# Feed-forward: the rounding offset finished by a second ScalarE pass instead of VectorE's clamp

## The reference

```python
def fp4_quant_dequant(x):               # blocks of 16 along the last dim
    xb = x.reshape(shape[:-1] + (shape[-1] // BLOCK, BLOCK))
    scale = jnp.max(jnp.abs(xb), axis=-1, keepdims=True) / 6.0
    scale = jnp.maximum(scale, jnp.float32(1e-12))
    xn = xb / scale
    idx = jnp.searchsorted(_MID, jnp.abs(xn))       # _MID = .25 .75 1.25 1.75 2.5 3.5 5
    q = _GRID[idx] * jnp.sign(xn) * scale           # _GRID = 0 .5 1 1.5 2 3 4 6
...
gate = fp4_linear(x, w_gate)            # fp4_linear: both operands through fp4_quant_dequant
y = fp4_linear(x, w_up)
h = jax.nn.silu(gate) * y               # 352 columns
return fp4_linear(h, w_down)
```

## Time and profile before

| | us |
|---|---|
| median of 3 runs | 813.99 |
| lowest, highest | 813.62, 816.39 |
| the profiled execution | 816.01 |
| its span, first to last instruction | 814.3 |
| VectorE busy | 540.7 (66%) |
| TensorE busy | 615.5 (76%) |
| ScalarE busy | 302.3 (37%) |
| POOL busy | 280.1 (34%) |

### The profile page before, as it was taken

The page is one execution under the profiler, slowest core; times in us unless marked ns, Lnnn a source line. Parts: engine busy times, 40 slices in busy tenths (PEclk is TensorE's granted clock), DMA queues, the critical chain, the costliest instruction groups (busy, mean ns, idle before and its releaser), DMA issues.

```text
span 814.3 us, 14007 instructions
## 1 busy us (share of the span) xinstructions
PE 615.5 (76%) x5231; PEld 445.5 (55%) x5231; DVE 540.7 (66%) x1126; ACT 302.3 (37%) x555; POOL 280.1 (34%) x328
## 2 busy tenths in 40 slices
PE   2376887888766667679777787798988988676886
PEld 1275875666633334378555565455655655454554
DVE  7615564333249948938889986666667666878784
ACT  2231111333224313412555545344444434455442
POOL 6540000000010000004558777534444445446454
PEclk9565998999989878969899998799999998899898
DMA  8400000000000000000000000000000000000000
GB/s 253 122 1 1 0 1 0 1 1 0 1 1 1 0 1 1 1 1 1 1 0 1 1 2 0 1 2 1 2 2 2 2 2 1 1 14 27 13 27 27
DMA packets 13676, 10.48 MB, mean 13 GB/s; under 512 B 1398, under 2 KB 12598, under 8 KB 13492
## 3 DMA queue, kind: packets, MB, share of 16 engines
q1 hardware_dynamic: 13620, 9.73, 4.2%
HBM read 7.63 MB, written 2.10 MB: 12 GB/s over the span
## 4 chain that ended last, share of the span: by engine, by line
PE 46%; DVE 21%; issue 14%; POOL 11%; ACT 7%; ACTq 0%; DMA 0%; POOLq 0%; DVEq 0%
PE ps L1157 6%; PE ps L1243 5%; PE ps L1374 4%; PE ps L1184 4%; PE ps L1272 3%; POOL G L276 3%; PE ps L1311 3%; DVE r L820 3%; PE ps L1393 2%; PE ps L1290 2%; PE ps L1193 2%; DVE S L828 2%; DVE arena L1017 2%; PE ps L1201 2%; POOL zT L279 1%
## 5 line engine op out<-in xcount | busy, mean ns | idle before, releaser
L1311 PE MATMUL ps<-wdT,xnt 128*128 128x128 f32 (+1 forms) x384 | 58.8, 310 | 45.5 <-ACT xnt L560 45.5
L1311 PEld LDWEIGHTS ps<-wdT,xnt 128*128 128x128 f32 (+1 forms) x384 | 52.5, 216 | 53.7 <-ACT xnt L560 53.3
L276 POOL TENSOR_TENSOR G<-S,hoff 128x704 f32<-128x704 f32 x32 | 48.6, 1518 | 80.5 <-DVE S L931 80.5
L1243 PE MATMUL ps<-G,xw 128*126 128x512 f32 x72 | 47.3, 810 | 30.1 <-ACT xw L505 22.4
L326 POOL TENSOR_TENSOR ln<-mv,lnc 128x4 f32<-128x4 f32 x64 | 13.0, 202 | 153.1 <-DVE mv L700 153.1
L345 POOL MEMSET early<- 128x2560 f32 x2 | 4.5, 2231 | 173.9 <-PE ps L1228 163.6
L553 ACT ACTIVATE xnt<-ps 128x352 f32<-128x352 f32 x64 | 29.7, 463 | 90.9 <-PE ps L1290 90.7
L365 POOL TENSOR_SCALAR_AFFINE_SELECT arena<-arena 128x1024 f32<-128x1024 f32 x32 | 34.9, 1092 | 71.5 <-ACT arena L637 71.5
L1017 DVE TENSOR_TENSOR arena<-ps,tri 128x1024 f32<-128x1024 f32 x32 | 39.2, 1225 | 23.4 <-PE ps L1374 23.4
L1290 PE MATMUL ps<-wguT,xnt 128*128 128x352 f32 x128 | 53.8, 503 | 1.0
L1292 PE MATMUL ps<-wguT,xnt 128*128 128x352 f32 x128 | 51.5, 485 | 3.9 <-DVE S L931 3.9
(11 more groups left out here) (199 smaller groups left out, 1525.0 us busy)
## 6 DMA issues: line engine op xcount, KB each, us to landing
X<-in_x SPq DMA_DIRECT2D x8, 256.0 KB, 4.9
out<-X SPq DMA_DIRECT2D x8, 256.0 KB, 2.3
wqkv<-in_wqkv SPq DMA_DIRECT2D x1, 1024.0 KB
band<-in_band SPq DMA_DIRECT2D x1, 897.8 KB
early<-in_wfc SPq DMA_DIRECT2D x1, 512.0 KB
kI<-in_scaled_eye SPq DMA_DIRECT2D x1, 192.0 KB
wattn<-in_wattn SPq DMA_DIRECT2D x1, 192.0 KB, 6.9
S<-in_wd SPq DMA_DIRECT2D x1, 176.0 KB, 3.6
```

The lines of the kernel that those rows point to most:

```text
L276: tt(out=hgrid, in0=hmoved[k], in1=hoff[k][:, :], op=ALU.subtract).then_inc(s["fh_grid"], 1)
L1243: last = mm(ps[0:WI, w, :], xw[:, w * WO:w * WO + WI], G1[:, b, :], start=True, stop=True)
L1311: last = mm(ps[:, T_BANK + 1, k * P:(k + 1) * P], hT[r % 2][0:FK[c], k, c, :], wdT[0:FK[c], c, :], start=(c == 0), stop=(c == 2))
```

## The change

The clamp on VectorE (L898) goes for both x and h. In its place ScalarE makes the offset in two passes: the first writes Square(SQ * v), which is RND * v^2 / 6, into the bf16 tile; the second reads that tile, adds RND * 4 / 3 by Identity with a bias from `lnc[:, 3]`, and writes it back in place. Between the two ScalarE waits for a semaphore that it raises itself. VectorE's move then waits for the second pass. The weights' offset (L426, L729), which is made once, stays as it was.

```diff
@@ ScalarE @@
-                    act(xoff[:, :], ps[:, X_BANK, :], ACT.Abs, scale=RND).then_inc(s["fx_abs"], 1)
+                    act(xoff[:, :], ps[:, X_BANK, :], ACT.Square, scale=SQ).then_inc(s["fx_offset"], 1)
+                    a.wait_ge(s["fx_offset"], 2 * n + 1)
+                    act(xoff[:, :], xoff[:, :], ACT.Identity, bias=lnc[:, 3:4]).then_inc(s["fx_offset"], 1)
...
-                    act(hoff[r % 2][:, :].rearrange("p (k n) -> p k n", k=2), up_banks(r), ACT.Abs, scale=RND).then_inc(s["fh_abs"], 1)
+                    act(hoff[r % 2][:, :].rearrange("p (k n) -> p k n", k=2), up_banks(r), ACT.Square, scale=SQ).then_inc(s["fh_offset"], 1)
+                    a.wait_ge(s["fh_offset"], 2 * n + 1)
+                    act(hoff[r % 2][:, :], hoff[r % 2][:, :], ACT.Identity, bias=lnc[:, 3:4]).then_inc(s["fh_offset"], 1)
@@ VectorE @@
-                def clamp(name, off, n):
-                    v.wait_ge(s[name + "_abs"], n + 1)
-                    ts(out=off[:, :], in0=off[:, :], scalar1=RND_MIN, scalar2=None, op0=ALU.max).then_inc(s[name + "_offset"], 1)
...
-                    clamp("fx", xoff, n)
-                    v.wait_ge(s["fx_offset"], n + 1)
+                    v.wait_ge(s["fx_offset"], 2 * n + 2)
...
-                    clamp("fh", hoff[r % 2], n)
-                    v.wait_ge(s["fh_offset"], n + 1)
+                    v.wait_ge(s["fh_offset"], 2 * n + 2)
```

## The result

| | before | after |
|---|---|---|
| median, us | 814.33 (4 runs, 813.62 to 816.39) | 863.40 (4 runs, 862.91 to 863.71) |
| ratio, with its 95% interval | | 1.0598 [1.0577, 1.0618] |
| span of the profiled execution, us | 814.3 | 861.9 |

The account below looks back on a forecast made before the run. The prediction took the loop of waits between TensorE and ScalarE, not VectorE, to bound the kernel. It summed 814.0 + 32.9 us of delay from the passes + 10 us of clock falls to 857 us, range 842 to 874.

Parts of the forecast that it names:

- The ring: Feed-forward loops: TensorE to silu, offsets, copy L560, back to TensorE; claimed to set steps, 6.28 us even, 7.15 odd.
- The bounds of -7 to +3 us: Uncertainty of the added ScalarE time, from cheaper or dearer passes, over 31 h and 10 x passes.
- the list: Feed-forward steps where the added passes delay TensorE, with the delay in each: sum 32.9 us.
- What the passes delay: ScalarE's queue ahead of copy L560: 16.8 us even steps, 7.9 and 6.5 odd and last, 1.7 steps 0 and 1.
- the 0.39 and 0.28 us of waiting for the ratio: Some odd steps, first and second loop: h offset waits for VectorE's L922; claimed to go with the clamp.
- The clock: TensorE's longer gaps before L1311 make its granted clock fall more often: 6.5 more falls, +10 us.
- the likeliest case: The forecast itself, with 6 to 13 clock falls: 852 to 863 us, chance 0.46.
- I take half: Gaps before L1311: 9.5 falls taken, between 11 at 3 in 5 and 6 at 3 in 9.
- VectorE as the bound: Rival: 19.8 us of clamps leave the path, passes lie in ScalarE's idle time; 794 us, chance 0.06.
- the difference alone: Rival: on a ratio, offset, clamp, move path, only passes less clamp count, 21.8 us; 836 us, chance 0.08.
- no more falls: Rival: bursts after TensorE's gaps keep the clock, no more falls than today; 847 us, chance 0.22.
- A fall in nearly every gap: Rival: the clock falls after nearly all 19 gaps above 2.5 us, +24.8 us; 872 us, chance 0.13.

Follow-up runs that it names:

- e3: Changed kernel with VectorE's two clamps put back behind the second pass, where they change no value: 863.05 us, ratio 1.058.
- e4: Kernel before with one Square pass in place of Abs and no clamp, so the offset is unfinished: 804.42 us, ratio 0.9849.
- e1: Kernel before with the two ScalarE passes for h alone; x keeps Abs and the clamp: 849.97 us, ratio 1.0395.
- e2: Kernel before with the two ScalarE passes for x alone; h keeps Abs and the clamp: 829.74 us, ratio 1.0167.
- e9: Changed kernel with ScalarE's copy L560 moved between the h passes and the x passes or normalisations: 814.95 us, ratio 0.9985.
- e10: Kernel before with copy L560 moved between the h offset and the x offset or normalisations: 802.18 us, ratio 0.9816.
- e8: Kernel before with ScalarE's copy L560 moved ahead of the offsets of the same step: 814.17 us, ratio 0.997.

## Why the prediction was right, and where it was off

- *What bounds.* Right. The ring of TensorE and ScalarE set the steps, not VectorE, although it was the busiest engine of that stretch. e3 and e4 show it from both sides.
- *First pass.* Right: 751 ns for Square and 753 for Abs on h; 583 against 601 on x. That difference is not the function's: Square takes 601 in e4, and Abs takes 582 in e1, where a second h pass runs before it as in the changed kernel.
- *Second pass.* 882 and 722 ns measured, 875 and 723 forecast from the shapes that differ in one thing each. The chain: L583 starts 0.79 us after L581 (465.33 to 466.12) and L573 0.78 after that, 1.57 in place of 0.63. That is 0.94 for h, with 0.92 forecast. For x it is 0.61 and 0.63, 1.24 in place of 0.48: 0.76. The bounds of -7 to +3 us count 31 h passes; the list has 28 without steps 0 and 1 and 32 with them, which moves the bounds by half a microsecond.
- *What the passes delay.* Right. Even steps 7.93 (7.96 forecast), odd ones 8.08 (8.07) in both loops, so the 0.39 and 0.28 us of waiting for the ratio did go. Between the first and last down projections the ring's part of the sum is 8.4 + 7.9 = 16.3 us in the first loop and 8.4 + 6.5 = 14.9 in the second. Measured were 28.7 and 18.8 with the clock; the clock's part of them, below, is 12.7 and 4.0, which leaves 16.0 and 14.8. Steps 0 and 1 cost 0.85 us per loop, 0.86 forecast.
- *The clock.* The mechanism was right, the size too small. 13 of 19 steps had a fall, at the edge of the 6 to 13 of the forecast, where 9.5 was taken. They cost 1.4 us in odd steps and 1.7 in even ones, one 2.8, together 20.9 us, where the three falls before cost 4.7; step 2 of both loops adds 0.5 (5.0 for 4.5). So the clock took 16.7 us and not 10, and that is nearly all that lies between 857 and 863. With 863.4 the time is just above the 852 to 863 of the likeliest case. The term that was too small is "I take half": it weighed the nine even gaps of before alike, although the gaps in question, 2.89 and 3.15 us, were all to be longer than any of them. It also left out step 2, where the trace of before has a fall in both loops, behind gaps of 2.71 and 3.11 us:

```profile
406.11 2.93 PE L1311 MATMUL ps<-wdT,xnt 128*128 128x128 f32 x12 [2.71 <-ACT xnt L560]
...
706.79 2.93 PE L1311 MATMUL ps<-wdT,xnt 128*128 128x128 f32 x12 [3.11 <-ACT xnt L560]
```

With these two it is 5 falls in 7 gaps of over 2.5 us, which for 19 gaps is 14. The upper bound of 24.8 us takes 1.55 us a fall, while the 1.5 worked out there (7.79 - 6.28 = 1.51) gives 24.2.
- *Sum.* 32.9 + 16.7 = 49.6 against 49.1 measured between the medians. That it meets this closely is in part luck: between the two profiled executions there are 47.6 us, and they are 30.8 of the ring, 1.7 of steps 0 and 1, 16.7 of the clock in the loops, 1.3 of the clock in the last down projection, and some -2.8 in the stages outside, which no term of the sum stands for.
- *Rivals.* No table load was added: L553 loads twice as before. VectorE as the bound is ruled out by e3, the difference alone by e1, and "no more falls" (847) by the trace of after. "A fall in nearly every gap" (872) was not reached, though e1's nine gaps of 3.15 us show that it can be so.
- *What would show it.* The waits of the down projection came to 76.7 us, 75 forecast. VectorE waits in front of the move, 59.6 us. The h offset's wait for the ratio went from 9.1 to 7.8 us and not to nothing: none of it is left in steps 2 to 14, 2.1 us are in steps 0 and 1 of each loop and 3.7 in the second loop's step 15.

What stays open: why six of the nine 3.15 us gaps of the changed kernel were followed by a fall and all nine of e1. The length of the gap alone does not decide it: in e3 four of nine gaps of 3.15 us were followed by a fall, and eight of ten of 2.86. How the gaps lie in time differs, 16.92 us for two steps in e1 and 17.4 to 20.2 in the changed kernel, but that this is the reason is argued and not shown. Open too is the spread of e2's runs.

## What to carry to other kernels

The busiest engine need not set the time: follow which copy or result the idle engine waits for, and read what stands ahead of it in its engine's queue. A pass added to an engine that was idle 20 of 50 us cost its full length plus the lost overlap in nearly every step, since it stood between a result and the copy that TensorE waited for; moving that copy ahead of the work that nobody waits for gave back as much as the change cost, and 1.8% on the kernel before. Work taken off an engine that waits is worth nothing, and a longer gap in front of matmuls can cost half as much again by the clock.

## What the runs showed of the hardware

- The granted clock fell in the matmuls behind TensorE gaps of 2.9 to 3.2 us in 13 of 19 cases in the changed kernel and 12 of 19 in e3, and behind those of 3.15 us in 9 of 9 in e1. Behind 2.11 us it fell in 0 of 10 in e1, behind 1.96 and 2.23 in 2 of 19 in e2, and never in steps 3 to 12 of e9 and e10, where the gaps are 1.74 us at most. The gap just ahead is not all that counts: e8 has a fall behind 0.69 us (467.64, a burst of 2.26 us), and step 2 of e10 one in each loop behind 1.59. A fall cost 1.4 to 1.7 us (once 2.8) in a loop whose step is 6 to 8 us.
- Filling the gaps with products that nobody uses left no fall in the filled steps (clock 0.98 for 0.83 over 100 us) and made the slower kernel 18.5 us faster, the faster one 0.5%.
- An activation in place on bf16 in SBUF with a pointer bias took 882 ns at 704 and 722 at 512 columns, 0.83 ns a column; from PSUM without a pointer it is 0.79 a column (753 and 601 ns). A wait for its own engine's previous instruction cost 0.04 us and the 0.12 us by which two activations otherwise overlap.
